# Heads' attention of a fused graph-attention and mixture-of-experts layer on one core: the masked copies of keys and queries move to VectorE

## What is computed

```
qkv = x @ wi.T + bi
q, k, v = split(qkv, 3)                       # each batch: 128 tokens x 128 features
q, k, v = heads(q), heads(k), heads(v)        # 16 heads of 8 features
scores = einsum('bhqd,bhkd->bhqk', q, k) / sqrt(8)
attn = softmax(scores, axis=-1)
o = einsum('bhqk,bhkd->bhqd', attn, v)
x = layernorm(x + o @ wo.T + bo)
```

## Time and profile before

| | us |
|---|---|
| median of 3 runs (631.16 to 636.73) | 632.66 |
| the profiled execution, its own time | 632.18 |
| its span in the trace | 630.4 |
| TensorE busy, matmuls | 547.7 (87% of the span) |
| VectorE busy | 454.8 (72%) |
| ScalarE busy | 395.6 (63%) |
| GpSimd busy | 269.9 (43%) |

### The profile page before, as it was taken

How to read it: one execution, slowest core, us unless ns; L and a number is a source line. 1 busy time by engine, 2 the same in 40 slices (tenths; PEclk the granted TensorE clock), 3 DMA queues, 4 the chain that set the end, 5 groups by cost and what they waited for, 6 DMA issues and landing times. The chain is left out here.

```text
span 630.4 us, 13793 instructions
## 1 busy us (share of the span) xinstructions
PE 547.7 (87%) x4346; PEld 361.5 (57%) x4346; DVE 454.8 (72%) x1189; ACT 395.6 (63%) x1097; POOL 269.9 (43%) x472
## 2 busy tenths in 40 slices
PE   5987999999999999998899987988887764888992
PEld 3565666667767666654445544554454443656781
DVE  4758777888778778857546879787887647865673
ACT  2513777777777777776576675656655542746781
POOL 0841122322222222011551566667484343765684
PEclk9998999999999999999999999999998976979996
DMA  9400000000000000001000010101220103144330
GB/s 365 198 1 2 1 2 2 2 0 0 0 0 0 0 0 0 1 1 34 3 1 2 2 35 18 53 1 53 107 89 10 44 18 104 60 137 132 99 98 14
DMA packets 15422, 26.56 MB, mean 42 GB/s; under 512 B 2416, under 2 KB 12661, under 8 KB 14598
## 3 DMA queue, kind: packets, MB, share of 16 engines
q1 hardware_dynamic: 12006, 18.96, 9.1%
q0 software_dynamic: 2784, 6.37, 2.9%
q10 hardware_dynamic: 576, 0.53, 0.2%
HBM read 18.29 MB, written 8.01 MB: 42 GB/s over the span
## 5 line engine op out<-in xcount | busy, mean ns | idle before, releaser
L1349 DVE TENSOR_REDUCE nm<-SC 128x8 f32<-128x1024 f32 x64 | 75.3, 1218 | 30.9 <-PE SC L914 27.1
L1268 DVE TENSOR_REDUCE room_w<-SC 128x512 f32<-128x2048 f32 x32 | 73.3, 2290 | 22.0 <-PE SC L787 22.0
L1822 ACT ACTIVATE room_p<-ST 128x1024 f32<-128x1024 f32 x64 | 61.9, 1019 | 18.6 <-PE ST L932 18.6
L532 POOL TENSOR_TENSOR spread<-parts,units 128x48 bf16<-128x48 bf16 x32 | 8.8, 275 | 146.5 <-DVE parts L1258 146.5
L1735 ACT ACTIVATE room_w<-room_w,shift 128x128 f32<-128x128 f32 x128 | 49.7, 390 | 21.7 <-DVE shift L1275 21.7
L1829 ACT ACTIVATE room_w<-SC 128x512 f32<-128x512 f32 x32 | 19.1, 597 | 49.3 <-PE SC L951 46.4
L684 POOL DMA_INDIRECT out<-room_v,id_r x39 | 39.7, 1017 | 21.7 <-POOL id_r L678 7.5
L1726 ACT ACTIVATE room_w<-ST,cv 128x128 f32<-128x128 f32 x128 | 36.4, 367 | 18.6 <-PE ST L802 18.6
L594 POOL DMA_INDIRECT sorted_rows<-room_w,slot_i x32 | 32.0, 999 | 34.8 <-issue 27.1
L547 POOL TENSOR_TENSOR ctx_t<-room_w 128x512 f32<-128x512 f32 x24 | 30.5, 1270 | 31.7 <-PE SC L787 31.7
L927 PE MATMUL ST<-room_v,room_w 32*128 32x512 f32 x256 | 36.5, 638 | 7.3 <-issue 5.7
(11 more groups left out here) (274 smaller groups left out, 1444.5 us busy)
## 6 DMA issues: line engine op xcount, KB each, us to landing
room_v<-sorted_rows SPq DMA_DIRECT2D x39, 130.0 KB, 2.1
ctx_t<-adj SPq DMA_DIRECT2D x1, 2048.0 KB, 11.2
x_t<-xT SPq DMA_DIRECT2D x1, 2048.0 KB, 15.6
room_w<-mask SPq DMA_DIRECT2D x1, 2048.0 KB, 19.8
room_w<-x SPq DMA_DIRECT2D x8, 256.0 KB, 2.9
w<-weights SPq DMA_DIRECT2D x1, 1292.0 KB, 6.8
x_t<-w SPq DMA_DIRECT2D x1, 1032.0 KB
ctx_t<-w SPq DMA_DIRECT2D x1, 1024.0 KB
```

The source lines that it names most:

```text
L1268: dve.tensor_reduce(logit[:, :, :], SC[:, :, :].rearrange("p b (i m) -> p b m i", i=TYPES), AX_X, ALU.max)\
L1349: dve.tensor_reduce(nm[:, v % 2, 2 * PER_R * pair:2 * PER_R * (pair + 1)], SC[:, 2 * pair:2 * pair + 2, :].rearrange("p r (i n) -> p (r i) ...
L1822: act.activation(ex[:, v % 2, 2 * pair:2 * pair + 2, :], ST[:, 2 * pair:2 * pair + 2, :], ACT.Exp)\
```

## The change

All masked copies are made on VectorE by one pair of functions, `mask_keys` and `mask_queries`, which take the group and the copies. In the step of batch `b` they come last in VectorE's order: at b = 0 and 1 two copies of the keys of group g+1 each, at b = 2 and 3 two copies of its queries each. GpSimd's and ScalarE's functions are gone, and TensorE waits for one semaphore, `qm_ready`, in place of `qm_pool` and `qm_act`. The arithmetic is the same multiplication.

```diff
@@ GpSimd
-            def mask_keys(g, heads):
-                pool.wait_ge(S("key_ready"), g + 1)
-                for i in heads:
-                    pool.tensor_tensor(k_m[:, g % 2, i, :], k_s[:, g % 2, :],
-                                       C("hmask")[:, i:i + 1].broadcast_to([128, GT]), ALU.mult)\
-                        .then_inc(S("km_ready"), 1)
-            def mask_queries(g):
...
-                if b == 0 and more and nxt > 0:
-                    mask_keys(nxt, (0, 1, 2))
...
-                if b == 1 and more and nxt > 0:
-                    mask_keys(nxt, (3,))
-                    mask_queries(nxt)
@@ TensorE, turned_scores
-                    pe.wait_ge(S("qm_pool"), 2 * (g + 1))
-                    pe.wait_ge(S("qm_act"), 2 * (g + 1))
+                    pe.wait_ge(S("qm_ready"), PER_R * (g + 1))
@@ VectorE
-            def first_keys():
-                dve.wait_ge(S("key_ready"), 1)
-                for i in range(PER_R):
-                    dve.tensor_scalar(k_m[:, 0, i, :], k_s[:, 0, :], C("hmask")[:, i:i + 1], None, ALU.mult)\
+            def mask_keys(g, heads):
+                dve.wait_ge(S("key_ready"), g + 1)
+                for i in heads:
+                    dve.tensor_scalar(k_m[:, g % 2, i, :], k_s[:, g % 2, :], C("hmask")[:, i:i + 1], None, ALU.mult)\
                         .then_inc(S("km_ready"), 1)
...
+            def mask_queries(g, heads):
+                dve.wait_ge(S("query_ready"), g + 1)
+                for i in heads:
+                    dve.tensor_scalar(q_m[:, g % 2, i, :], q_s[:, g % 2, :], C("hmask")[:, i:i + 1], None, ALU.mult)\
+                        .then_inc(S("qm_ready"), 1)
...
                 if b == 3 and whole:
                     norm1_variance(done)
+                if more and nxt > 0:
+                    if b < 2:
+                        mask_keys(nxt, (2 * b, 2 * b + 1))
+                    else:
+                        mask_queries(nxt, (2 * b - 4, 2 * b - 3))
@@ ScalarE
-            def mask_queries(g):
-                act.wait_ge(S("query_ready"), g + 1)
-                for i in (2, 3):
-                    act.activation(q_m[:, g % 2, i, :], q_s[:, g % 2, :], ACT.Copy, scale=C("hmask")[:, i:i + 1])\
-                        .then_inc(S("qm_act"), 1)
...
-                    if more and nxt > 0:
-                        mask_queries(nxt)
```

More of the change, by code:

```diff
@@ L1312, in step @@
                 if isinstance(t, int) and g == G - 3:
-                    first_keys()
+                    mask_keys(0, range(PER_R))
                 if ahead(t, g, 2):
@@ L1512, in _ @@
             value_out(0, X0)
-            first_queries()
+            mask_queries(0, range(PER_R))
             dve.tensor_copy(before_h[:, :], C("before")).then_inc(S("halves_ready"), 1)
```

## The result

The changed kernel takes 638.32 us (median of 18 runs, 636.26 to 643.16); the kernel before took 631.12 us in the runs beside it (626.6 to 636.73). The two medians differ by 7.2 us; the ratio is 1.0131 with a 95% interval of 1.0108 to 1.0153, which is 6.8 to 9.7 us: slower by about 1%, clear of noise. The forecast was 644 with a range of 635 to 651. The profiled execution has a span of 637.9 us, against 630.4.

A forecast was written before the change was run, and what follows sets the result against it. The prediction took TensorE's attention loop (turned_scores, ScalarE's exponentials, weigh, turns) to bound the kernel. Waits net of relief, +5.8 us, and clock falls, +6, gave +11.8 on 632.66: 644 us, range 635 to 651.

The forecast's parts named there:

- rival A: TensorE's waits come but its clock stays at the upper level: 638.5 us; chance 0.2.
- Item 1: End of fourth step: next group's first turned_scores waits 2.25 us for VectorE's second query pair, about 1.5 before group 1.
- Item 2: End of first step: first key pair adds 0.88 us to VectorE's chain, covered by 2.2 us of relief; costed at nothing.
- Item 3: End of second step: second key pair delays the next scores by 1.3 us; third step grows 0.5 to 7.96 us.
- Item 4: End of third step: first query pair delays the fourth step's row maxima to 3.3 us, weigh by 0.4; step 6.5.
- The relief: Removing GpSimd's and ScalarE's copies shortens first, second and fourth steps; 2.6 us per group, undisturbed first 6.1, second 6.15.
- The sum of the steady group: The four steps of a steady group add up to 28.96 us; four such groups 115.8 against 113.2, +2.6.
- The clock: TensorE's clock falls behind four of six 2.25 us waits, 1.5 us each: +6 us, bounds 0 and 9.
- B: Faster: VectorE finishes its tail before the next group's turned_scores is due, without that wait 623.5 us; chance 0.05.
- C: Second key copy comes behind a GpSimd operation and waits 1.27 us in five groups, +6.4: 650.8 us; chance 0.1.

The follow-up runs named there:

- e1: Changed kernel with only the second query pair moved ahead of normalise at b = 3; 621.27 us, ratio to before 0.9878.
- e5: Changed kernel with VectorE's copies for groups 1 to 7 cut to 4 of 512 columns; 629.01 us, ratio to before 0.9969.
- e4: Kernel before with GpSimd's six copies per group cut to 4 of 512 columns, ScalarE's two whole; 622.36 us, ratio 0.988.
- e8: Kernel before with ScalarE's two query copies per group cut to 4 of 512 columns, GpSimd's whole; 627.31 us, ratio 0.9961.
- e2: Changed kernel with both query pairs ahead of normalise and the second key pair earlier at b = 1; 619.09 us, ratio to before 0.9811.
- e3: Changed kernel with nine unused matmuls on TensorE ahead of the first turned_scores of groups 1 to 7; 633.85 us, ratio to before 1.0032.
- e6: e2 with the first query pair right behind the third step's row maxima, beside a running GpSimd operation; 618.19 us, ratio to before 0.9832.
- e7: e2 with ScalarE's layer norm output (norm1_out) moved behind the exponentials of b = 2; 624.07 us, ratio to before 0.9914.

## Why the prediction was right, step by step

The direction and the range held, and the mechanism with them. The total was forecast at +11.8 and measured at +7.2 us. That number, 638.3, is nearer to rival A's price (638.5) than to the forecast (644), and by itself it would have spoken for A; that is chance. The clock did fall, for about 3 us net in place of 6, and the groups without it came out about 1.5 us below their 5.8.

- *Item 1, the second query pair.* Forecast 2.25 us, 1.5 for the first; the profile has 2.13 to 2.25 and 1.29. Undoing it alone (e1) brought 17 us. e5 splits it nearly as the forecast did: 1.26 us of tail and hand-over where 1.39 was forecast, and 0.88 of copies.
- *Item 2, the first key pair.* Costed at nothing; the row maxima of the second step start at 2.32 us (389.00 - 386.68), undisturbed. Right.
- *Item 3, the second key pair.* Scores forecast 2.43 us after L927, measured 2.46; third step forecast 7.96, measured 7.98. The number is right and its reason half so: by e4, 0.28 us of the 0.5 comes with the shorter second step and not with the copies, which add only 7.98 - 7.74 = 0.24. In the last of the seven groups the item was put at nothing, since `cond` is missing. The same step with the granted clock at 1.00, without the late key copies (e8) and with them (the changed kernel):

```profile
474.86:481.53 6.67, 4.91 (x70) 3.15 (x70) 5.50 (x17) 4.47 (x9) 4.48 (x7) 1.00 0.00 1
```

```profile
481.08:488.49 7.41, 5.34 (x72) 3.02 (x71) 5.75 (x19) 4.71 (x9) 4.70 (x8) 1.00 0.00 0
```

  It grew by 0.74 us. How much of that is the keys is open, for with the key pair early it is 7.41 too (e2).
- *Item 4, the first query pair.* Row maxima forecast at 3.3 us, measured 3.05; fourth step forecast 6.5, measured 6.33. The term was 0.2 too large per group: L1485, the L1507 of before, ends 2.35 us into the step as forecast, but the pair begins 0.09 ahead of that end and the maxima 0.79 behind the pair's start, where the forecast added 0.93.
- *The relief.* First step forecast 6.1, second 6.15; measured 6.04 and 6.05. e4 shows the mechanism. e8 corrects one part of its reading: in front of groups 3 to 6 the 0.6 of the fourth step is real only together with the rest.
- *The sum of the steady group.* 28.96 forecast, 28.63 measured where the clock held, so the four groups were forecast 1.3 us too long.
- *The clock.* This is the term that was mis-sized. Four falls at 1.5 us made +6. In the profile three of the six long waits were followed by a spell at the lower level, costing 1.23, 1.23 and 2.17 us, 4.6 in all, and e3 measures 4.5 to 6.2. And the profiled execution of the kernel before has a fall of its own among these groups, at 1.5 us, which the forecast used for its price and forgot to take off: the trace of the changed kernel has no fall in that step. Net of it the clock brought about 3 us, not 6. The rest, forecast at 5.8, is by the same account 2.7 (e3) + 1.5 = 4.2, and by the windows of the seven groups with the falls taken out 0.99 + 1.86 + 1.31 + 0.33 = 4.5. Which steps the clock falls in changes from one trace to the next, so each of these sums is good to 1 us or so.

Of the rivals, A (the clock holds) is the state of e3 and not of the change. B failed as it should: the waits were as long as the rows said, and its other side, that the relief without the wait would make the kernel clearly faster, is e1 and e2. C's mechanism exists (e6), and its condition was not met: the pair was over 0.09 us before L582 began.

## What to carry to other kernels

Work that is put last in an engine's step inherits that step's whole tail: before moving it there, look up when the tail ends against the start of its reader, not how long the work is, since here even copies of 4 columns made the reader wait 1.6 us, and the same whole pair one place earlier, inside an idle time, made the kernel 1.2% faster than before (e1), three pairs 1.9% (e2). When work leaves one engine for another, count what the first engine was holding up (here VectorE's small operations, by 0.8 to 0.9 us each) apart from what the second one is charged. And when a forecast takes the price of a disturbance from the kernel before, that disturbance is already in the time before, and comes off.

## What was not expected of the hardware

- A VectorE `tensor_scalar` of 128x512 in float32 with one tensor input waited for a GpSimd operation that had started 0.1 us before it: 1.46 us instead of 0.48 (e6). In e7 even a cast of 8 columns took 0.88 us beside one, against 0.25 in e2.
- Waits of TensorE of nearly the same length, 2.13 to 2.25 us in one execution, were followed by a spell at the lower clock in three cases (2.23, 2.23, 2.25) and by none in three others (2.13, 2.14, 2.21). In e5 it was one of six, behind 1.82 and not behind 1.79; in the kernel before the clock fell behind an idle of 1.76 us and not behind 1.84. No single length divides them all.
- ScalarE's 1.3 us per group, removed from in front of a chain that TensorE plainly waited for, moved the wait to the next step: wholly at two of the four starts of groups 3 to 6 (13.96 us for the two steps around batch 16, with and without), and all but 0.2 us of it at the others.
